# Three edits to a fused four-stage transformer kernel: first query products, routing before the shared expert, and a paired down product

## The reference

```
x = x + tanh(g_xattn[0]) * L0_xattn(ctx, layernorm(x))   # top-76 of 256 similarities per row, symmetrised, mixed with x
x = x + tanh(g_ffn[0])   * L0_ffn(layernorm(x))          # 16 blocks of 64 hidden units, 4 chosen per token, gelu
x = x + tanh(g_xattn[1]) * L1_xattn(layernorm(x), ctx)   # 16 heads, latent queries of 192, rope, softmax
x = x + tanh(g_ffn[1])   * L1_ffn(layernorm(x))          # routed experts plus one shared expert

# L1_xattn: q_big = rope((x Wq) w_kc_q);  scores = (q_big W_qr)(kv W_kr)^T
# L1_ffn:   scores = sigmoid(x router_w^T); 3 of 8 groups, 4 of 32 experts per token; capacity 40 per expert
#           Y = (silu(Xp W_gate) * (Xp W_up)) W_down per expert, weighted, scattered back onto the tokens
#           shared = (silu(x shared_gate^T) * (x shared_up^T)) shared_down^T
```

## Time and profile before

| what | value |
|---|---|
| median of three runs | 491.15 us |
| the profiled execution | 489.43 us, span 487.6 us |
| PE busy | 445.3 us (91% of the span), 2744 instructions |
| DVE, ACT, POOL busy | 307.2, 245.6, 188.1 us |
| chain that ended last | PE 15%, DMA 5% (XR gathers 5%), DVE 2% of the span |
| DMA | 59651 packets, 42.48 MB |

### The profile page before, as it was taken

One profiled execution on the slowest core, in us unless ns is written; L12 is line 12 of the kernel. 1 busy time (PEld: TensorE's weight loads), 2 busy tenths in 40 slices (PEclk: granted clock), 3 DMA queues, 4 the chain that ended last, 5 costly groups with the idle time before them and its releaser, 6 DMA issues. The chain is left out here.

```text
span 487.6 us, 8840 instructions
## 1 busy us (share of the span) xinstructions
PE 445.3 (91%) x2744; PEld 289.0 (59%) x2744; DVE 307.2 (63%) x899; ACT 245.6 (50%) x606; POOL 188.1 (39%) x190
## 2 busy tenths in 40 slices
PE   5897999898685999999999999999997996998997
PEld 2676877786422555555555555555675754655686
DVE  3988799943245757667776767677545567455511
ACT  3685444536203776766676676766673330133300
POOL 3452404132215556475554666656532003443000
PEclk9997999999979999999999999999999998699999
DMA  8644100000023223443434342222002990279202
GB/s 253 200 105 115 39 0 1 1 2 1 0 54 84 70 48 76 93 109 71 103 73 101 82 97 65 65 65 65 24 2 76 310 285 11 59 191 318 81 1 87
DMA packets 59651, 42.48 MB, mean 87 GB/s; under 512 B 22449, under 2 KB 52706, under 8 KB 59618
## 3 DMA queue, kind: packets, MB, share of 16 engines
q1 hardware_dynamic: 58850, 39.71, 31.0%
q0 software_dynamic: 768, 2.36, 2.1%
HBM read 27.24 MB, written 2.23 MB: 60 GB/s over the span
## 5 line engine op out<-in xcount | busy, mean ns | idle before, releaser
L1117 POOL TENSOR_TENSOR PB<-PB,inv 128x512 f32<-128x512 f32 x64 | 66.5, 1039 | 81.7 <-DVE inv L1179 81.5
L1054 ACT ACTIVATE PB<-ps,low 128x256 f32<-128x256 f32 x128 | 59.5, 470 | 31.5 <-DVE low L1173 31.5
L1112 POOL TENSOR_TENSOR RO<-RO,TC 128x512 f32<-128x512 f32 x48 | 61.0, 1271 | 33.3 <-DMA RO<-TS 17.8
L1173 DVE TENSOR_REDUCE low<-ps 128x2 f32<-128x512 f32 x64 | 44.1, 689 | 39.6 <-PE ps L969 39.0
L399 POOL TENSOR_TENSOR HT<-GL,MS 128x512 f32<-128x512 f32 x16 | 20.3, 1276 | 63.3 <-ACT MS L671 61.2
L1145 DVE TENSOR_TENSOR TS<-ps,sinq 128x512 f32<-128x512 f32 x48 | 33.2, 691 | 16.5 <-PE ps L945 12.2
L977 PE MATMUL ps<-ident,PB 128*128 128x128 f32 x256 | 41.1, 283 | 1.7 <-POOL PB L1117 0.8
L977 PEld LDWEIGHTS ps<-ident,PB 128*128 128x128 f32 x256 | 27.7, 140 | 24.6 <-issue 20.7
L1062 ACT ACTIVATE PTS<-ps 128x512 f32<-128x512 f32 x64 | 38.2, 597 | 7.2 <-PE ps L977 5.1
L945 PE MATMUL ps<-XH,CH 128*128 128x512 f16 x96 | 37.6, 392 | 2.6 <-POOLq L1105 2.6
L945 PE MATMUL ps<-XL,CH 128*128 128x512 f16 x96 | 37.4, 390 | 0.0
(11 more groups left out here) (232 smaller groups left out, 888.1 us busy)
## 6 DMA issues: line engine op xcount, KB each, us to landing
RO<-TS SPq DMA_DIRECT2D x64, 128.0 KB, 2.3
RO<-TS SPq DMA_DIRECT2D x64, 64.0 KB, 2.0
EGU<-in_L_ffn_W_gate_dram SPq DMA_DIRECT2D x10, 384.0 KB, 5.9
...
```

The costliest lines, as they stand in the source:

```text
L1054: e = act.activation(PB[t % 2][:, h, :], g.ps[:, SC + t % 2, h * S:(h + 1) * S], ACT.Exp, bias=low[:, t % 2, h:h + 1], scale=-1.0, accum_o ...
L1112: pool.tensor_tensor(RO[:, n, x, :], RO[:, n, x, :], TC[x][:, :], ALU.add).then_inc(sum_ok, 1)
L1117: pool.tensor_tensor(PB[t % 2][:, :, :], PB[t % 2][:, :, :], inv[:, t % 2, :].unsqueeze(2).broadcast_to([P, 2, S]), ALU.mult).then_inc(nor ...
L1173: dve.tensor_reduce(low[:, t % 2, :], g.ps[:, SC + t % 2, :].rearrange("p (h s) -> p h s", h=2), AX.X, ALU.min).then_inc(low_ok, 1)
```

## The change

Three parts, made together.

**First query groups.** Folding of pair 1 (`fold(6)` to `fold(11)`) leaves the first stage. In the first stage's last batch PE makes pair 0's first three query products (`first_queries`), DVE rotates them, SP swaps, POOL adds (between its `masked` products), and after the last `result` PE makes the first context product, which ACT and DVE split. The second stage's prologue now folds pair 1 and makes queries 3 to 5 of pair 0, alternating. The weights of pair 3 are loaded in the second stage. Tiles are laid over each other to make room: w1 and w2 lie in `rot`, which later holds RO, TC and TS; `turned` holds CTT and V and later one HT. On DVE `rest(B - 3)` moves ahead of `first(B - 1)`.

**Logits first.** All router logits come before `shared_rows`. ACT loads its sigmoid table early with a one-element activation, and keeps the up half in UPS, so that POOL instead of DVE multiplies the shared expert's halves. `shared_rows(2)` and `(3)` stand where PE waited for DVE's lists; `shared_down` stands after the indices.

**Paired down, dense tiles.** `down` runs once a pair with two 64-column products; the hidden rows are copied by ACT into HX instead of by DVE into HP. The results stay in YS, one tile a pair, and SP packs them with 40 DMAs (33 for pairs 0 to 12, 7 for the rest) into ten dense tiles of 128 slots; the scatter has 8 x 10 x 2 products and waits for the packing. The slot tokens go through DRAM and one transpose. Gathers run four ahead instead of three.

```diff
+def rotate_query(dve, g, q, k, bank):
+
+    x = k % QT
+    dve.wait_ge(g.q_ps, GROUPS_Q * q + (k + 1))
+    dve.wait_ge(g.sum_ok, GROUPS_Q * q + (k - QT + 1 + SUM0))
+    batches = lambda y: y.rearrange("p (b s) -> p b s", b=2)
+    over = lambda y: y[:, x // 2, :].unsqueeze(1).broadcast_to([P, 2, S])
+    src = batches(g.ps[:, bank, :])
+    dve.tensor_tensor(batches(g.TS[x][:, :]), src, over(g.sinq), ALU.mult).then_inc(g.sin_ok, 1)
+    dve.tensor_tensor(batches(g.TC[x][:, :]), src, over(g.cosq), ALU.mult).then_inc(g.rope_ok, 1)
...
+def context_product(pe, g, q, u, n):
+
+    pe.wait_ge(g.sum_ok, GROUPS_Q * q + (QT * n + QT + SUM0))
+    pe.wait_ge(g.qc_ok, 2 * q + (n + QC0))
+    for h in range(2):
+        pe.matmul(g.ps[HI[h], QP, :], g.M[u][:, h, :], g.RO[:, n, h, :], start=True, stop=False)
+    for h in range(2):
+        mm = pe.matmul(g.ps[HI[h], QP, :], g.M[u][HI[h], 2, :], g.RO[HI[h], n, 2, :], start=False, stop=True)
+    mm.then_inc(g.qc_ps, 1)
...
-                for r in range(2, 4):
-                    sp.wait_ge(filled, N_FOLD + FOLDS * (r - 1))
-                    load_pair(sp, g, i, r, r % 2)
+                sp.wait_ge(filled, N_FOLD + FOLDS)
+                load_pair(sp, g, i, 2, 0)
+                for k in range(QT):
+                    swap_partners(sp, g, 0, k)
...
                     for n in range(UNITS):
                         masked(b, n)
+                        if b == B - 1 and n >= 1:
+                            add_partners(pool, g, 0, n - 1)
...
+                def first_queries(k):
+
+                    pe.wait_ge(xl_ok, 2)
+                    pe.wait_ge(fold_b, 2)
+                    pe.wait_ge(g.rope_ok, k + ROPE0)
+                    query_product(pe, g, 0, k, QA)
...
-                    if b == 0:
-                        for k in range(FOLDS, 2 * FOLDS):
-                            fold(k)
...
+                        if b == B - 1 and n < QT:
+                            first_queries(n)
...
+                pe.wait_ge(gelu_ok, UNITS * B)
+                context_product(pe, g, 0, 0, 0)
                 second_norm(B - 1)
...
+                rest(B - 3)
                 first(B - 1)
                 norm_inverse(dve, g, n1, B - 1)
                 norm_apply(dve, g, n1, B - 1)
-                rest(B - 3)
                 second(B - 2)
                 route(B - 1)
+                dve.wait_ge(g.d_ropeq, ROPE_LOADS)
+                dve.wait_ge(g.sin_sign, 3)
+                rotate_query(dve, g, 0, 0, QA)
                 norm_inverse(dve, g, n2, B - 2)
                 norm_apply(dve, g, n2, B - 2)
+                rotate_query(dve, g, 0, 1, QA)
                 rest(B - 2)
+                rotate_query(dve, g, 0, 2, QA)
                 second(B - 1)
                 norm_inverse(dve, g, n2, B - 1)
                 norm_apply(dve, g, n2, B - 1)
+                context_rest(dve, g, 0, 0, 0)
                 rest(B - 1)
...
-                for k in range(GROUPS_Q):
-                    queries(0, 0, k)
-                to_context(0, 0, 0)
+                for f in range(FOLDS):
+                    fold(1, 1, f)
+                    if f < QT:
+                        queries(0, 0, QT + f)
                 pairs(pe, step, cross)
...
+                def pack(q):
+
+                    sp.wait_ge(yl_ok, q + 1)
+                    for h in range(2):
+                        for row, at, size in pieces(2 * q + h):
+                            sp.dma_start(YP[at % P:at % P + size, at // P, :, :],
+                                         YS[q][DC * h + row:DC * h + row + size, :, :]
+                                         ).then_inc(d_pack[0 if q < EARLY else 1], 16)
+
+                for q in range(PAIRED):
+                    for n in range(RING, ST_T):
+                        if pair_of(n - RING) == q:
+                            sp.wait_ge(y_ps, q + 1)
+                            weights(n)
+                    pack(q)
...
+                def shared(n):
+
+                    h, o = shared_steps[n]
+                    pool.wait_ge(sl_ok, 2 * n + 2)
+                    pool.tensor_tensor(HS[:, o, 512 * h:512 * h + 512], SL[n % 2][:, :], UPS[n % 2][:, :],
+                                       ALU.mult).then_inc(hs_ok, 1)
+
+                shared(0)
+                shared(1)
                 pool.wait_ge(sg_ok, 1)
...
+                shared(2)
+                shared(3)
                 pool.wait_ge(d_rows, 16 * (B + 2))
                 pool.wait_ge(idx_ok, 1)
                 for q in range(PAIRED):
                     if q >= FLIGHT:
                         pool.wait_ge(d_g[q % FLIGHT], 16 * (q // FLIGHT))
-                    if q >= 3:
-                        pool.wait_ge(xg_ok, q - 2)
+                    if q >= 4:
+                        pool.wait_ge(xg_ok, q - 3)
                     pool.indirect_dma_start(XR[q][:, :], None, rows_dram[:, :],
...
-                shared_rows(0)
                 logits(0)
                 logits(1)
+                logits(2)
                 turn_normed(B - 1)
-                logits(2)
                 logits(3).then_inc(rl_ps, 1)
-                for n in range(1, 4):
-                    shared_rows(n)
+                shared_rows(0)
+                shared_rows(1)
 
                 pe.wait_ge(mk_ok, 1)
                 for t in range(NT):
@@ -1437,16 +1527,15 @@
                     mm = pe.matmul(g.ps[E * quarter:E * quarter + E, KEYB, j * P:(j + 1) * P], MKb[:, t, :],
                                    g.keys[:, t, :], start=True, stop=True)
                 mm.then_inc(key_ps, 1)
-                pe.wait_ge(hs_ok, 2)
-                for t in range(4):
-                    shared_down(t)
-
-                pe.wait_ge(hs_ok, 3)
+                shared_rows(2)
+
+                pe.wait_ge(sl_ok, 6)
                 pe.wait_ge(top_ok, 2 * LISTS - 1)
                 for a in range(QUART):
                     mm = pe.matmul(g.ps[0:E, LISTB, a * CAP:(a + 1) * CAP], g.ident[:, E * a:E * a + E], top[:, :],
...
-                def down(n):
-                    m = CAP * count(n)
-                    pe.wait_ge(hp_ok, pair_of(n) + 1)
-                    if n >= 2:
-                        pe.wait_ge(yl_ok, n - 1)
+                def down(q):
+
+                    pe.wait_ge(hp_ok, q + 1)
+                    if q >= 2:
+                        pe.wait_ge(yl_ok, q - 1)
                     else:
-                        pe.wait_ge(sh_ok, n + 3)
-                    flat = HP[:, :, :].rearrange("p j w -> p (j w)")
-                    for j in range(count(n)):
-                        at = EPT * (n % 2) * (SLOTS + CAP) + SLOTS * j
-                        mm = pe.matmul(g.ps[0:m, Y + n % 2, 0:D], flat[:, at:at + m],
-                                       ED[n % RING][:, j, :], start=(j == 0), stop=(j == count(n) - 1))
+                        pe.wait_ge(sh_ok, q + 3)
+                    for h in range(2):
+                        e = 2 * q + h
+                        mm = pe.matmul(g.ps[DC * h:DC * h + DC, Y + q % 2, 0:D], HX[q % 2][:, DC * h:DC * h + DC],
+                                       ED[e // EPT % RING][:, e % EPT, :], start=True, stop=True)
                     mm.then_inc(y_ps, 1)
...
-                    for n in DOWN_AT[q]:
-                        down(n)
-                for n in DOWN_AT[PAIRED]:
-                    down(n)
+                    if q == 1:
+                        pe.wait_ge(d_eb, 48)
+                        pe.wait_ge(sh_ok, 3)
+                        pe.transpose(g.ps[:, Y, 0:TILES_S], slot_raw[:, :],
+                                     g.ident[0:TILES_S, 0:TILES_S]).then_inc(slot_ps, 1)
+                        pe.wait_ge(tok_ok, 1)
+                    if q >= 1:
+                        down(q - 1)
+                down(PAIRED - 1)
 
...
-                pe.wait_ge(st_ok, ST_T)
+                pe.wait_ge(st_ok, TILES_S)
                 pe.wait_ge(h_ok, PAIRED)
-                pe.wait_ge(yl_ok, ST_T - 1)
-                for t in range(4):
-                    for n in range(ST_T - 1):
+                pe.wait_ge(d_pack[0], N_PACK[0])
+                for t in range(NT):
+                    for n in range(FULL):
                         scatter(t, n)
-                pe.wait_ge(yl_ok, ST_T)
+                pe.wait_ge(d_pack[1], N_PACK[1])
                 for t in range(NT):
-                    for n in range(ST_T - 1 if t < 4 else 0, ST_T):
+                    for n in range(FULL, TILES_S):
                         mm = scatter(t, n)
                     mm.then_inc(acc_ps, 1)
 
...
+                    act.activation(UPS[n % 2][:, :], g.ps[:, 2 * (n % 2) + 1, :], ACT.Copy).then_inc(sl_ok, 1)
 
                 for q in range(B):
                     norm_root(act, g, n3, q)
+                    if q == B - 1:
+                        act.activation(primed[:, :], g.gate[0:1, 0:1], ACT.Sigmoid)
                     if q >= 1:
```

(12 more changed lines are left out.)

332 lines of the change are left out of this document (158 added, 174 removed).

## The result

| kernel | median of its runs | ratio to before, 95% interval |
|---|---|---|
| before | 491.57 us (14 runs, 487.49 to 494.19) | |
| changed | 488.35 us (14 runs, 486.20 to 490.19) | 0.9936, 0.9914 to 0.9958 |

The change makes the kernel 3.2 us faster, where 9.3 were forecast; 488.35 us lies above the stated range (474 to 487.5). The profiled execution of the changed kernel took 488.47 us, near its median.

What follows compares the result with a forecast made beforehand. PE, 91% busy and mostly at 2.4 GHz, was taken as the bound. -3.1 - 4.0 - 7.0 + 4.6 - 1.8 + 1.5 + 0.5 = -9.3 gave about 481.8 us in the median, range 474 to 487.5.

Steps and rivals of the forecast that it cites:

- Part one, -3.1 us: First stage and second stage's prologue: first scores count as 151.1 us against 154.17, -3.1 us, bounds -6.5 and 0.
- Part two, -4.0 us: Routing up to the first gathered rows: indices 2.9 us earlier, rows turned at 417.3 us, -4.0 us, bounds -5 and +3.4.
- SG's last input is ready 1.0 us sooner: Routing: with the logits first, the sigmoid's last input comes 1.0 us sooner, one term of the 2.9 us.
- I take full clock: Indices to first gathered rows: PE at full clock, 7.8 us; half clock throughout would be 7.4 us more.
- rival B: Ahead of shared_rows(0) or through shared_down: PE falls to or stays at 1.2 GHz, +4 us, 485.8 us; chance 0.14.
- The loop, -7.0 us: Expert loop: PE's work falls from 39.78 to 33.0 us, loop 36.5 us instead of 43.5, bounds 0 and -10.5.
- the loop turns faster and the same weights pass; I take 3.5 us again: Expert loop: PE's waits stay at 3.5 us, 1.0 of it the new wait for slot tokens at pair 1.
- SP's queue, +4.6 us: Between loop and scatter: packing DMAs land at 458.4 us, so PE waits 4.6 us, bounds 0 and +22.
- At 0.62 each they are 9.3 us, at 1.90 28.5. I take the low end: SP's queue in the loop: the 15 weight DMAs were priced at 0.7 us each, 10.5 us.
- Rival C: Fourth stage: packing DMAs held up behind weight sets in SP's queue; 0.95 us an issue gives 496.4 us; chance 0.06.
- The scatter, -1.8 and +1.5; end, +0.5: Scatter: 160 products instead of 176, -1.8 us; start at 1.2 GHz, +1.5; X's updates and stores closer at the end, +0.5.
- D: Expert loop: gathers set the pace, loop keeps 43.5 us, packing ends beside it, 484.2 us; chance 0.13.

Runs made afterwards that it cites:

- ninth experiment: Changed kernel with the paired down and dense tiles undone, plus the last batch's turn put ahead of the previous batch's logits: 483.88 us, 0.9851 of before.
- twelfth experiment: Changed kernel with scatter in four groups, last turn first, slot tokens in the second bank, packing split between SP and POOL: 478.63 us, 0.9754 of before.
- experiment 8: Changed kernel with the paired down and dense tiles undone, plus a ring of seven weight sets instead of six: 485.46 us, 0.9873 of before.
- Experiment 4: Changed kernel without the 40 packing DMAs, the scatter multiplying the unpacked pair tiles: 481.86 us, 0.9828 of before.
- experiment 5: Changed kernel with the five weight sets loaded in the loop bringing one expert instead of three, same number of DMAs: 483.61 us, 0.9848 of before.
- experiments 3: The changed kernel as it is, measured again beside the others on the same chip: 488.68 us, 0.9957 of before.
- experiment 6: Changed kernel with the scatter in four groups of slot tiles, each waiting for its own packing alone: 483.80 us, 0.9842 of before.
- 10 to 12: On experiment 6's kernel: slot tokens turned into the second bank, 480.84 us; packing split between SP and POOL, 481.80 us; both with the ninth experiment's turn, 478.63 us.

## Why the prediction was wrong, point by point

- **Part one, -3.1 us.** Mechanism right, size too small. First scores at 149.84 us; "about 151" was forecast. The prologue began at 137.98 us instead of 138.6 and took 11.9 us instead of 12.5. The half clock came and cost 3.0 us, more than the 2.3 allowed, but the waits were 1.1 us and not 1.4, the work 7.8 us and not 8.3, and ACT's table load, for which 0.5 was added, started only at 150.36, behind the first scores. The ratios give more, 6.6 to 7.6 us (5.4 to 7.6 between the medians). 2 us of that is that the trace I summed against was faster than the kernel before is in the median; which stretches hold the rest stays open.
- **Part two, -4.0 us.** Half of it (2.3 us) came in this trace, and none in the medians on top of part one. The indices came 0.65 us sooner against the first scores, where 2.9 were forecast; 1.7 us came behind them. Two steps failed. "SG's last input is ready 1.0 us sooner": I counted the logits' new place and missed that the change puts the last turn behind `logits(2)`, whose input waits for ACT behind the early table load. The rows of the order in the section on the change show it. It cost half a microsecond against the first scores instead of gaining one, and the ninth experiment gets 1.9 us in the trace by undoing it, clock aside. "I take full clock" was right from the indices to the first gathered rows (7.2 us against 7.8), but rival B's mechanism struck where B had put it, ahead of `shared_rows(0)`: 6.8 us at half clock from about 386.2, behind a wait of 1.87 us, a gap of the size that the prediction had held against B. It costs 3.4 us, near B's 4. The second list also waits 1.18 us for ACT's second copy.
- **The loop, -7.0 us: the largest miss.** It came out at +2.4. Of the 9.2 us between 36.5 and 45.7, PE's work is 2.1 (35.1 us at full clock instead of 33.0: `down` cost 0.160 us an instruction in the twelfth experiment and not 0.136, and less of it overlaps its neighbours), the half clock in the loop 3.4 (6.8 us at 1.2 GHz behind a wait of 2.47 us), and waits 3.7: 7.2 us of idle time instead of 3.5, of which 3.3 are for sets and 1.9 for the slot tokens (1.0 was forecast). The failed sentence is "the loop turns faster and the same weights pass; I take 3.5 us again". Before, PE asked for a set every 4 us; at 2.2 us a pair it asks every 3.3 us. A set of 1.18 MB at the 284 GB/s that full engines moved in experiment 8, gathers included, takes 4.2, by my estimate, and the old pace just met it. Experiment 4 shows that bound by itself (a loop of 41.8 us), experiment 5 without it (39.8 us, no wait for sets), experiment 8 that it was no bound before.
- **SP's queue, +4.6 us: the step that decided.** It was named as what is late next, and was: the scatter waited 3.55 us for the packing. That looks like a hit and is luck: the loop that it was measured against was forecast 9 us shorter. From the first gathered rows to the scatter's start 41.1 us were forecast and 49.2 measured, and those 8.1 us are nearly all that the sum of -9.3 is off by against the traces (-0.9). Since the scatter waited for the queue, a loop of 36.5 us would have saved only what it took off the queue. "At 0.62 each they are 9.3 us, at 1.90 28.5. I take the low end ... since the packing leaves the queue time to drain" is the failed step: the queue took 39.2 us instead of 31.0. By count alone it takes 32.8 (experiment 5), so the count was priced nearly right, and the slow issues that come with the sets' bytes, 6.4 us, were not. The sum also hid a link: the packing stands in front of the sets, so a slow queue makes the loop slow, and not only the scatter late: by 1.6 to 3.0 us (experiments 3, 4, 6 and 10 to 12), half clock included, whose share stays open. I let it act only at the loop's end. Rival C had the right mechanism, with 0.95 us an issue; it was 0.82, just under the 0.85 from which C said the kernel is slower.
- **The scatter, -1.8 and +1.5; end, +0.5.** 19.29 us against 19.39 before, half clock included; 17.6 without it (experiment 6). Right. The end cost nothing.
- **D**, that gathers keep the loop at 43.5 us, had the loop's size about right (45.7) with the wrong resource, sets and not gathers (1.5 us of waits), and no wait ahead of the scatter.
